# The first attention group's maxima in two parts: short row tiles first, eleven long chunks ahead of the first scores, five behind them

## What is computed

```python
def _L0_attn_ref(x, Wq, bq, Wk, bk, Wv, bv, Wo, bo, J_attn, lambda_attn):
    ...
    Q = heads(Wq, bq); K = heads(Wk, bk); V = heads(Wv, bv)
    scores = jnp.einsum('bhid,bhjd->bhij', Q, K) / scale
    QJ = jnp.einsum('bhid,hde->bhie', jnp.tanh(Q), J_attn)
    delta = jnp.einsum('bhie,bhje->bhij', QJ, jnp.tanh(K))
    scores = scores + lambda_attn * delta
    causal = jnp.triu(jnp.ones((S, S), dtype=bool), k=1)
    scores = jnp.where(causal, -jnp.inf, scores)
    probs = jax.nn.softmax(scores, axis=-1)
    out = jnp.einsum('bhij,bhjd->bhid', probs, V)
...
h = _layernorm(x) * (1 + ca) + sa
x = x + ga * _L0_attn_ref(h, ...)
h = _layernorm(x) * (1 + cb) + sb
x = x + gb * _L0_ffn_ref(h, ...)          # norm, W1, relu, W2 of the row's expert
```

## Time and profile before

| | |
|---|---|
| median of 3 runs | 770.96 us (769.65 to 771.85) |
| the profiled execution, own time | 773.26 us |
| its span | 771.5 us |
| PE / DVE / ACT busy, share of the span | 88% / 71% / 65% |
| mean granted clock of PE | 0.96 |

### The profile page before, as it was taken

The page is one execution under the profiler, slowest core; times in us unless marked ns, Lnnn a source line. Parts: engine busy times, 40 slices in busy tenths (PEclk is TensorE's granted clock), DMA queues, the critical chain, the costliest instruction groups (busy, mean ns, idle before and its releaser), DMA issues.

```text
span 771.5 us, 15278 instructions
## 1 busy us (share of the span) xinstructions
PE 676.7 (88%) x5199; PEld 341.3 (44%) x5199; DVE 545.0 (71%) x1249; ACT 500.7 (65%) x1182; POOL 258.0 (33%) x342
## 2 busy tenths in 40 slices
PE   3657899999999998999999989999998989887693
PEld 2352344333333433433344434343443227886593
DVE  6959666887866786778667868788777603897352
ACT  1431577766767866766877586866767788655472
POOL 2009109200201943513138234210352202466443
PEclk9867699999999999999999999999999999999797
DMA  8996732456533251925606165636313445424610
GB/s 224 316 206 240 131 68 64 131 98 113 118 67 60 71 178 32 177 56 148 124 1 193 58 112 97 157 94 129 97 43 112 161 142 169 126 78 146 177 40 11
DMA packets 55572, 91.88 MB, mean 119 GB/s; under 512 B 10257, under 2 KB 26157, under 8 KB 55240
## 3 DMA queue, kind: packets, MB, share of 16 engines
q1 hardware_dynamic: 49308, 79.72, 41.6%
q0 software_dynamic: 3520, 8.42, 3.1%
q10 hardware_dynamic: 2668, 2.78, 1.3%
HBM read 51.04 MB, written 37.90 MB: 115 GB/s over the span
## 4 chain that ended last, share of the span: by engine, by line
PE 54%; DVE 20%; ACT 12%; issue 7%; DMA 4%; another core or an unknown queue 1%; ACTq 1%; DVEq 0%; POOL 0%; SPq 0%; POOLq 0%
PE PS L1232 15%; PE PS L1192 12%; PE PS L1258 11%; ACT arenaA L1014 7%; DVE PS L1672 6%; PE PS L1309 4%; PE PS L1320 3%; DVE block_max L1679 3%; ACT arenaB L932 2%; PE PS L1262 2%; DVE arenaA L1355 2%; DVE arenaB L1355 2%; PE PS L1197 1%; PE PS L1140 1%
## 5 line engine op out<-in xcount | busy, mean ns | idle before, releaser
L1014 ACT ACTIVATE arenaA<-PS 128x512 f32<-128x512 f32 (+3 forms) x768 | 332.4, 498 | 157.3 <-PE PS L1262 119.9
L1672 DVE CUSTOM_DVE_ANT_0 PS<-PS,mask 128x1024 f32<-128x1024 f32 (+3 forms) x256 | 261.4, 1035 | 90.4 <-PE PS L1192 85.4
L1258 PE MATMUL PS<-arenaA 99*128 99x512 bf16 (+3 forms) x768 | 221.5, 332 | 14.9 <-ACT arenaA L1014 11.6
L1192 PE MATMUL PS<-arenaA 96*128 96x512 bf16 (+3 forms) x768 | 198.8, 335 | 26.0 <-DVE maxima L1672 8.2
L1258 PEld LDWEIGHTS PS<-arenaA 99*128 99x128 bf16 x768 | 71.6, 97 | 202.5 <-ACT arenaA L1014 141.6
L1232 PE MATMUL PS<-arenaA,Vs 128*9 128x512 f32 (+3 forms) x1536 | 158.3, 488 | 0.0
L1679 DVE TENSOR_REDUCE block_max<-PS 128x8 f32<-128x1024 f32 (+1 forms) x96 | 100.4, 1045 | 28.8 <-PE PS L1197 26.1
L1192 PEld LDWEIGHTS PS<-arenaA 96*128 96x128 bf16 x768 | 66.7, 100 | 90.9 <-DVE maxima L1672 31.3
L1262 PE MATMUL PS<-after,identb 128*128 128x128 bf16 x512 | 104.5, 221 | 0.0
L1063 ACT ACTIVATE arenaA<-PS,b1p 128x128 f32<-128x128 f32 x184 | 52.6, 374 | 35.3 <-PE PS L1309 21.2
L831 POOL DMA_INDIRECT out_dram<-arenaA x46 | 46.1, 1002 | 82.7 <-DVE arenaA L1355 73.8
(11 more groups left out here) (219 smaller groups left out, 691.1 us busy)
## 6 DMA issues: line engine op xcount, KB each, us to landing
arenaA<-k_parts SPq DMA_DIRECT2D x96, 128.0 KB, 8.0
arenaA<-by_expert SPq DMA_DIRECT2D x46, 192.5 KB
o_raw<-OT SPq DMA_DIRECT2D x32, 256.0 KB, 2.1
k_parts<-arenaB SPq DMA_DIRECT2D x24, 256.0 KB, 3.8
arenaA<-q_parts SPq DMA_DIRECT2D x16, 384.0 KB, 5.2
q_parts<-arenaB SPq DMA_DIRECT2D x18, 256.0 KB, 3.8
arenaA<-in_L_ffn_W_dram SPq DMA_DIRECT2D x2, 2048.0 KB, 12.9
arenaA<-q_parts SPq DMA_DIRECT2D x16, 256.0 KB, 5.7
```

Source lines behind the costliest of these rows:

```text
L1014: a.activation(PT[:, u % EB, h, off:HALF], PS[:, 4 + n % SB_, off:HALF], ACT.Exp).then_inc(exp_ok, 1)
L1192: last = mm(PS[:, place + c0 // HALF, at:at + c1 - c0], SQ(g, h)[0:KROWS, t * P:(t + 1) * P], SK(g, h)[0:KROWS, c0:c1], start=(at == 0), s ...
L1258: last = mm(bank[:, off:HALF], SK(g, h)[0:MROWS, kb * P:(kb + 1) * P], SQ(g, h)[0:MROWS, qc * HALF + off:(qc + 1) * HALF], start=True, sto ...
L1672: v.tensor_tensor_reduce(out=src, in0=src, in1=mask[:, S - n:S], scale=1.0, scalar=-3e38, op0=ALU.add, op1=ALU.max, accum_out=maxima[:, pl ...
```

## The change

The short chunks of group 0 come first. Their maxima are reduced into a tile of their own (`first_max`), turned by an item of their own ("H") and sent by four DMAs, one a row tile. The first 16 slots of scores need no more than that. Of the 16 long chunks 11 stand ahead of the first score, and 5 behind the slots 0, 0, 1, 1, 2. The chunks 0 to 5 of group 1 and the T of group 0, formerly ahead of the first score, stand behind the slots 3 to 10, and the long maxima go by four more DMAs, awaited before slot 16. Five projections of the next sequence (X0, X1, Q0, Q1, K0) move to the slots 9 to 14. The weights are turned two pieces behind each of the first five chunks, where it was one behind each of ten. SP loads the stacks of group 2 ahead of the long maxima, those of group 3 behind them. ACT's eight norm steps stand in the slots 0 to 7, where they stood in every other of the slots 0 to 15.

```diff
+        first_max = sb("first_max", [P, HG * TB])
...
-        FIRST = [... ("X0", "X1", "K0", "K1", "Q0", "Q1", "J0", "J1", "V0", "V1")] + [("m", 0, k) for k in range(NM)] + \
-                [("m", 1, 0), ("m", 1, 1), ("T", 0, 0)] + [("m", 1, k) for k in range(2, EARLY)]
+        SHORT = [k for k in range(NM) if CHUNKS[k][1] < 4]
+        LONG = [k for k in range(NM) if CHUNKS[k][1] >= 4]
+        AHEAD_LONG = 11
+        FIRST = [... as before ...] + [("m", 0, k) for k in SHORT] + \
+                [("m", 0, LONG[0]), ("H", 0, 0)] + [("m", 0, k) for k in LONG[1:AHEAD_LONG]]
+        HALF_SLOTS = 16
+        SOON = {"X0": 9, "X1": 10, "Q0": 12, "Q1": 13, "K0": 14}
+        LATER = dict(K1=1, V0=4, V1=7, J0=11, J1=13)
+        OPENING = [(n, "m", 0, k) for n, k in zip((0, 0, 1, 1, 2), LONG[AHEAD_LONG:])] + \
+                  [(3, "m", 1, 0), (4, "m", 1, 1), (5, "T", 0, 0)] + [(5 + k, "m", 1, k) for k in range(2, EARLY)]
...
-                for i in range(NU * HG):
+                for i in range(opens, NU * HG):      # opens = 16 in the first group
...
+            def send_short_maxima():
+                sp.wait_ge(max_used, FIRST.index(("H", 0, 0)) + 1 + MB_)
+                for t in range(4):
+                    sp.dma_start(stacks[KROWS:MROWS, 0, 0, :, t * P:(t + 1) * P], mrow[HG * TB + t:P:TB, :]).then_inc(m_short, 16)
+            def send_long_maxima(use):
+                sp.wait_ge(max_used, use + 1 + MB_)
+                for t in range(4, TB):
+                    sp.dma_start(stacks[KROWS:MROWS, 0, 0, :, t * P:(t + 1) * P], mrow[HG * TB + t:P:TB, :])\
+                        .then_inc(m_in if t == TB - 1 else m_short, 16)
...
-            send_maxima(0, T_FIRST)
+            send_short_maxima()
             sp.wait_ge(w_out, 32)
             for g in range(2, NG):
                 ones(g)
                 load_group(0, g)
+                if g == 2:
+                    send_long_maxima(dve_use("first", 0, ...))
...
-                        steps.setdefault((0, t // 2), []).append((1 + 2 * (t % 2), lambda b, t=t: norm_rows(b, t), 1))
+                        u, h = (t // 4, t % 4) if body == "first" else (t // 2, 1 + 2 * (t % 2))
+                        steps.setdefault((0, u), []).append((h, lambda b, t=t: norm_rows(b, t), 1))
...
-                for _ in range(6 if i == len(PREP) - 1 else 1 if i >= len(PREP) and turned_weights < 16 else 0):
+                for _ in range(6 if i == len(PREP) - 1 else min(2, 16 - turned_weights) if i >= len(PREP) else 0):
...
-                        if u == 0:
+                        if gi == 0 and u == 0:
+                            pe.wait_ge(m_short, 4 * 16)
+                        if gi == 0 and u == HALF_SLOTS // HG:
+                            pe.wait_ge(m_short, 7 * 16)
+                        if u == (HALF_SLOTS // HG if gi == 0 else 0):
                             pe.wait_ge(m_in, (gi + 1) * 16)
...
+                if k == SHORT[-1] and group == 0:
+                    dve.wait_ge(max_used, done)
+                    v.tensor_reduce(short_rows(first_max[:, :]), block_max[:, place % 2, :, :, :], AX.X, ALU.max).then_inc(short_max, 1)
```

More of the change, by code:

```diff
@@ L219, in build @@
         PREP_AT = tuple(10 + (37 * k) // 20 for k in range(len(PREP)))
[L220 to L221 removed]
+        SHORT = [k for k in range(NM) if CHUNKS[k][1] < 4]
+        LONG = [k for k in range(NM) if CHUNKS[k][1] >= 4]
+        AHEAD_LONG = 11
+        FIRST = [("P", 0, PREP.index(step)) for step in ("X0", "X1", "K0", "K1", "Q0", "Q1", "J0", "J1", "V0", "V1")] + [("m", 0, k) for k in SHORT] + \
+                [("m", 0, LONG[0]), ("H", 0, 0)] + [("m", 0, k) for k in LONG[1:AHEAD_LONG]]
[4 more added lines that the diff above has]
+                  [(3, "m", 1, 0), (4, "m", 1, 1), (5, "T", 0, 0)] + [(5 + k, "m", 1, k) for k in range(2, EARLY)]
+        assert len(LONG) == 16
+        OPENING = sorted(OPENING + [(n, "P", 0, PREP.index(step)) for step, n in SOON.items()], key=lambda it: it[0])
         SLOT_COST = [70 * (kb >= 4 * qc) + (HALF - max(0, kb - 4 * qc) * P) * 0.87 for qc, kb in UNITS for h in range(HG)]
@@ L256, in build, with schedule @@
         BEST_IN = dict(middle=2, last=1)
-        def schedule(prep, post, last):
+        def schedule(prep, post, last, opening=()):
             groups, n = [], 0
@@ L263, in schedule @@
                 seq = list(SEQ)
+                fixed = opening if g == 0 else ()
                 extra = [(at, "P", k) for k, at in enumerate(PREP_AT)] if g == 0 and prep else []
+                if fixed:
+                    extra = [(at, "P", PREP.index(step)) for step, at in LATER.items()]
                 extra += post.get(g, ())
@@ L271, in schedule @@
                 early = 0.82 if last and g == NG - 2 else 1.0
-                pace = early * (sum(SLOT_COST) + sum(c[1] for c in cost)) / max(1, sum(c[0] for c in cost))
+                opens = HALF_SLOTS if fixed else 0
+                pace = early * (sum(SLOT_COST[opens:]) + sum(c[1] for c in cost)) / max(1, sum(c[0] for c in cost))
                 slots, clock, m = [], 0, 0
-                for i in range(NU * HG):
+                for i in range(opens, NU * HG):
                     clock += SLOT_COST[i]
@@ L280, in schedule @@
                 items = []
-                for m, (kind, ahead, k) in enumerate(seq):
-                    items.append((n, slots[m], kind, (g + ahead) % NG, ahead, k))
+                for at, kind, ahead, k in list(fixed) + [(slots[m], *it) for m, it in enumerate(seq)]:
+                    items.append((n, at, kind, (g + ahead) % NG, ahead, k))
                     n += kind != "D"
@@ L285, in schedule @@
             return groups, n
-        BODIES = dict(first=schedule(True, STATS_AT, False), middle=schedule(True, POST_AT, False), last=schedule(False, POST_LAST, True))
+        BODIES = dict(first=schedule(True, STATS_AT, False, OPENING), middle=schedule(True, POST_AT, False), last=schedule(False, POST_LAST, True))
         N0 = len(FIRST)
@@ L468, in _ @@
                 load_group(0, g)
+                if g == 2:
+                    send_long_maxima(dve_use("first", 0, next(it[0] for it in BODIES["first"][0][0] if it[2] == "T")))
             def by_head(b):
@@ L515, in attention @@
                     if body != "last" or g + 1 < NG:
-                        t_use = next(it[0] for it in BODIES[body][0][g] if it[2] == "T")
+                        t_use = next(it[0] for it in BODIES[body][0][g] if it[2] == "T" and it[4] == 1)
                         send_maxima((g + 1) % NG, dve_use(body, b, t_use))
@@ L1176, in maximum @@
                     return
-                if kind == "T":
-                    pe.wait_ge(row_max, group + 1)
+                if kind in "TH":
+                    pe.wait_ge(*((row_max, group + 1) if kind == "T" else (short_max, 1)))
                     for at in range(0, P, HG * TB):
-                        last = mm(PS[at:at + HG * TB, bank, 0:P], maxima[:, g, :], ident[:, :], start=True, stop=True)
+                        last = mm(PS[at:at + HG * TB, bank, 0:P], maxima[:, g, :] if kind == "T" else first_max[:, :], ident[:, :], start=True, stop=True)
                     last.then_inc(max_ps, 1)
@@ L1183, in maximum @@
                 heads, t = CHUNKS[k]
-                if k == 0:
+                if k == 0 or loads == 0 and g == 0 and k == SHORT[0]:
                     pe.wait_ge(stack_in[g], (loads + 1) * 9 * 16)
@@ L1386, in _ @@
             v.memset(block_max[:, :, :, :, :], -3e38)
+            v.memset(first_max[:, :], 0.0)
+            short_rows = lambda columns: columns.rearrange("p (h t) -> p h t", h=HG)[:, :, 0:4]
             def batch_stats(b):
```

21 lines of the change are left out of this document (12 added, 9 removed).

## The result

The changed kernel takes 778.62 us, the median of 4 runs (776.97 to 780.78), and the kernel before, run beside it, 770.88 (769.65 to 771.85). The ratio is 1.0096, 95% interval 1.0077 to 1.0116: slower by 7.7 us, where I had forecast no change and a range that ended at 775.4.

What follows compares the result with a forecast made beforehand. DVE was taken to bound up to the first score, PE after it. The first score's nine us mostly go back; slot 16 plus 1.3, then 32.1 for 32.92: plus 0.5, 771.5 against 770.96, range 766.8 to 775.4.

Steps and rivals of the forecast that it cites:

- Step 1: Short chunks and weights from 51.78 us: DVE idles over 4 us more, has 1.6 of added work, ends at 65.75.
- Step 2: Ten long chunks ahead of the first score: DVE ends them at 76.5, first score at 75.0 instead of 84.22.
- Step 3: Slots 0 to 10: 12.0 us of DVE work takes most of the gain back; slot 16 at 95.6, 1.3 later.
- Step 4: Four DMAs of the long maxima, issued from 86.1, land at 92.1; slot 16 waits for nothing, 3.5 us to spare.
- the rival: Slower: long maxima queued behind group 2's loads land at 99.3, PE stands 3.9 us at slot 16; 774.4, chance 0.09.
- Step 5: Slot 16 to group 1's first score: 32.1 us instead of 32.92, so group 1 begins at 127.7 instead of 127.19.
- signs of being wrong: Forecast is wrong if the time beyond group 1's beginning differs by over a us, as nothing there has moved.
- slower: Cases of a slower time than forecast, chance 0.21 together: late long maxima, low clock, late short maxima.
- a low clock: Slower: mixing chunks into scores keeps PE from full clock, the case of the upper bound, 776.7; chance 0.08.
- late short maxima: Slower: short maxima, behind 2 MB of weights, land after 75.0 and hold up the first score; at 78, 774; chance 0.04.
- my law: Long chunks at low clock start 1.42 us (1024 columns) after the end of the one two before; low to about 81.
- the upper bound: Late full clock in the mixed slots adds 2.7 us beside the late chunks and 2.5 behind X1: 776.7.

Runs made afterwards that it cites:

- h1: Changed kernel with weights turned one piece behind each of ten chunks and all ten projections at their old places; 1.0030 to the kernel before.
- h3: As h1, but short and long chunks of group 0 alternate as before, all 16 long ones ahead of the first score; 1.0041 to the kernel before.
- f1: As h1, but with group 3's stacks and values loaded ahead of the long maxima; 781.0 us, 1.0145 to the kernel before.
- e1: Changed kernel with group 3's stacks and values loaded ahead of the long maxima; 1.0085 to the kernel before.
- e2: Changed kernel with the projections V0 and V1 moved back behind J1, near slots 32 to 36; 1.0088 to the kernel before.
- h4: The changed kernel again, nothing altered, on another chip; 778.5 us, 1.0093 to the kernel before.
- f2: Kernel before plus only the added work: item H with its reduction and split, and eight maxima DMAs for one; 1.0027 to the kernel before.
- e3: Changed kernel with all ten projections of the next sequence back at their old places; 1.0076 to the kernel before.
- e4: Changed kernel with one piece of weights turned behind each of ten chunks instead of two behind each of five; 1.0067 to the kernel before.
- f3: As f1, but short and long chunks of group 0 alternate as before, 11 long ones ahead of the first score; 1.0149 to the kernel before.
- f4: As f3, but all 16 long chunks of group 0 stand ahead of the first score; 1.0156 to the kernel before.

## Why the prediction was wrong, step by step

**Step 1, the front: near, in part by luck.** The split was to end at 65.75 and ends at 66.2. But the clock rose at 57.25 and not at 54.8, and PE was through with the short chunks at 62.4 and not at 61.65. And the terms do not add up to what I wrote: 61.65, 1.2, 0.22, 0.15, 0.75 and 1.30 make 65.3. The two errors offset each other. DVE waits among the short chunks as worked out:

```profile
53.07 0.69 DVE L1719 TENSOR_REDUCE block_max<-PS 128x4 f32<-128x512 f32 x1 [6.95 <-PE PS L1226]
55.57 0.96 DVE L1719 TENSOR_REDUCE block_max<-PS 128x6 f32<-128x768 f32 x1 [1.80 <-PE PS L1226]
57.89 1.22 DVE L1719 TENSOR_REDUCE block_max<-PS 128x8 f32<-128x1024 f32 x1 [1.37 <-PE PS L1226]
```

**Step 2, ten long chunks: right, 0.6 late.** First score at 75.58 for 75.0.

**Step 3, slots 0 to 10: the direction right, 1.8 too small.** I had slot 16 at 95.6 and it is at 97.40. Of this 0.6 comes from step 2; one more wait of PE for DVE, 1.01, was not counted. It is at the pair of chunks behind slot 0, which has no score in it, where my rule had one score between any two chunks:

```profile
77.33 0.93 PE L1221 MATMUL PS<-arenaA 96*128 96x512 bf16 x2 [1.01 <-DVE maxima L1712]
```

The condition "DVE without a pause of over 0.7 us from 66 to 90" is broken once by it: DVE's pause is 1.17 at 78.4. The central claim of the step held: a start 8.6 us earlier is lost again before slot 16. The reasons I gave, the same chunks on DVE and a low clock of PE, agree with the rows (DVE is busy for 13.53 us up to slot 16, where it was for 5.65 in the earlier trace rows, and the clock stood at 0.50 until 84.6), but no run takes either away.

**Step 4, the long maxima: right.** In the change they are issued from 87.5, and there is no wait at slot 16; h1 shows that the copies land within 6 us of the first issue when only group 2 is in front, and h3, which waited, 6.2. The mechanism of the rival is real, and f1 shows its price with group 3 in front too. The rule I cited, that each DMA engine takes a ring's descriptors in their order (the Trainium skill, DMA: Bandwidth & Descriptors, "Queues, rings and completion order"), agrees with f1: the copies, last in SP's queue, landed at 96.9, when the DMA engines had emptied.

**Step 5, slot 16 to group 1: failed, by 3.9 us.** Forecast 32.1, measured 36.04. Its terms:

- I had not seen a wait. PE 2.19 us, for the values of group 3. The step V0 was at 111.5 on DVE before and is wanted at 102.1 now, and the values land at 104.6. That the load stands behind the long maxima counts for little: it is issued 2.7 us later than before (95.51 for 92.78) and lands 0.3 later. I had followed SP's queue from the maxima's side alone, and counted the moved projections as work, without asking what each of them waits for. This wait is in the code, a condition deep in a helper (`later and half == 0`). That it is this DMA, the trace shows; that it can be removed, e1 and e2 show.
- Other waits of PE: 3.86 us in many pieces against 2.8 by my terms (the 1.73 of before, less 0.45, plus 1.0 for DVE and 0.5 for the turned maxima). The last was not there at all: PE has no wait for a DMA ahead of group 1. The larger pieces are for banks that ACT still holds from a projection (0.51, 0.76, 0.45 above), where I had let one of them go.
- Work: PE is busy for 29.99, where by my terms it would have been 29.3 (31.19 - 3.75 + 1.9): 4608 columns of chunks came to 2.7 rather than 1.9 (the chunks there take 10.07 for 7.35), the five projections to 4.26 rather than 3.75, and 0.3 is not accounted for. These pieces are counted from the start of an instruction to the start of the next, since the records overlap, and are good to some 0.2 us.

The three together: 2.19 + 1.1 + 0.65 = 3.9.

**The sum.** Slot 16 1.8 late and step 5 3.9: 5.7 us at group 1 (133.4 for 127.7). So the step that failed is step 5, which had no term for DVE's wait for the values and had the other waits 1.1 and the work 0.65 too low, and, by less, step 3. In the medians the account is another: h4 is 7.2 us above before, of which 4.9 go with the early projections and the two pieces a chunk taken back together (h1), and the 2.3 left are near the 2.1 of the added work (f2).

One of my signs of being wrong came true as well. Beyond group 1's beginning the changed kernel's profile is 1.7 us shorter than that of before (642.7 for 644.3), with the same order of PE; 1.1 of it lies behind the last score, where the profiles differ by 5 us and more among themselves with the same order of PE.

**What the early projections did** can be read between h1 and the change. In the change they stretch the way from first score to slot 16 from 17.80 to 21.82, 4.0 us, and shorten the way from slot 16 to group 1 from 38.00 to 36.04, 2.0 us. PE's work there does fall, by 4.4 (34.35 to 29.99), but its idle time rises by 2.4 (3.65 to 6.05), the wait for the values most of it. The front is 1.9 longer, for which the two pieces a chunk are the difference. 4.0 - 2.0 + 1.9 = 3.9, the distance of 133.4 and 129.5. The clock came back at 88.3 in h1 and at 84.6 in the change. Against e3, where it came back at 84.4 and the front is the same, the projections alone stretch the way to slot 16 by 4.6 (17.20 to 21.82) and shorten the next one by 2.1 (38.10 to 36.04).

**Chances.** I gave 0.21 to slower, with the mechanisms of late long maxima, a low clock and late short maxima. The first was absent. The third was absent in the change, but not far: where the front is shorter, the first score waits for the short maxima, 1.34 us in e4 and 0.51 in h1. For the second, the clock came back at 84.6 in the profiled execution, not far from the 81 of my law, and at 93 to 94 in e1 and e2. By the upper bound slot 16 would have been at 100.8 (95.6 + 2.7 + 2.5), and e2 has it at 99.5. So the bound was about right; but I had it as a case of its own, when the same order of PE shows either return in different profiles. It belonged into the range of every case.

**What stays open.** That the wait for the values costs the change time is shown only in its stretch, not in the total. How the 4.9 us between h1 and h4 are shared between e3's edit and e4's is not settled: alone they gave about 1.3 and 2.0 us against h4 by their ratios, on another chip, and are not told apart from nothing. By their ratios h1 to h3 lie 0.2, 1.3 and 1.1 us above f2, where their profiles have group 1 1.8, 1.8 and 0.7 us later; so an offset of one profile is good to about two us only. In e1's profile the part behind the last score took 138.7 us, where the others have 130 to 135, and nothing I read explains it. Whether e1 and e2 only happened to have their clock late, or have it late more often than the change, two profiles of either cannot say.

## What to carry to other kernels

When an instruction moves forward in an order, list every semaphore (the counter on which one engine or DMA releases another) that it waits for, also those that a helper waits for only in some cases, and find when the DMA behind each lands. Here it landed at the same time as before, and the step that needed it had moved 9.4 us forward. To start the busy engine earlier in a stretch that another engine bounds gained nothing here: of the 10.5 us by which h1's first score is earlier than before's, 2.8 are left at slot 16 and none at group 1. And the 2.8 are not a gain either, since five chunks of group 1 that before has behind it by then are still to come in h1: up to group 1 PE is busy there for 3.2 us more and idle for 1.9 more than in the earlier trace rows. What stayed is 2.3 us of loss, near the 2.1 that the added work costs by itself (f2). Small copies that somebody waits for go ahead of large loads in a queue: behind one group of loads they were in time or 0.8 us late, behind two PE stood for 6.6 to 8.8 us.

## What of the hardware I had not expected

The clock's return is not fixed by PE's order: with the same order up to slot 16 it came at 84.6, 85.6, 93.2 and 94.1 (the change, h4, e1, e2), and slot 16 at 97.4, 97.1, 98.7 and 99.5. A wait of 2.2 us was followed by a fall of the clock in h4 and by none in the first profile of the same kernel. The Trainium skill (TensorE: Matmul & The Clock Gate, "Why this matters for your kernels") tells to avoid idle gaps of PE between bursts of products, and means longer ones than this. The trace of h4, with 0.52 over the two us from 106, agrees with it in direction; that of the first profile shows nothing of it.

Four copies of 3 by 4 by 128 elements take 2.97 us to issue in SP's queue, 0.74 each, and landed 6.0 us or less after the first issue with one group of loads in front (h1; 6.2 in h3, which waited), but 11.8 to 12.6 us after it with two (f1, f3, f4).
